# Stacked f32r score products in the first attention, and the value products between the second and third group of turned tiles

## The reference, cut to what matters

```python
h = tok(x)                                   # patches @ W + b + pos_embed
h = concatenate([h, txt], axis=1)            # 1536 tokens x 64
n = layernorm(h)
q, k, v = n @ Wq + bq, n @ Wk + bk, n @ Wv + bv
h = h + softmax(q @ k.T) @ v                 # "attn0": one head of 64
```

## Time and profile before

| what | value |
|---|---|
| median of 3 runs | 5559.78 us (5559.76 to 5568.03) |
| the profiled execution's own time | 5535.23 us |
| its span, first to last instruction | 5533.4 us |
| mean granted TensorE clock | 0.834 of full speed |
| busy: PE, PEld, DVE, ACT, POOL | 78%, 52%, 60%, 34%, 9% of the span |

### The profile page before, as it was taken

The page is one execution under the profiler, slowest core; times in us unless marked ns, Lnnn a source line. Parts: engine busy times, 40 slices in busy tenths (PEclk is TensorE's granted clock), DMA queues, the critical chain, the costliest instruction groups (busy, mean ns, idle before and its releaser), DMA issues.

```text
span 5533.4 us, 72582 instructions
## 1 busy us (share of the span) xinstructions
PE 4295.1 (78%) x26536; PEld 2888.3 (52%) x26536; DVE 3325.1 (60%) x9075; ACT 1894.7 (34%) x3395; POOL 490.8 (9%) x820
## 2 busy tenths in 40 slices
PE   6886855699888855699888855699887855699987
PEld 4554634555646534555646534555646544555646
DVE  4444769555545769555545769555555769655555
ACT  2333522144332522144432522134432532234432
POOL 0110000011100000021100000021100000021100
PEclk9898865699988975699988975689998985699988
DMA  2000000000000000000000000000000000000000
GB/s 81 3 3 16 1 16 1 1 1 1 1 1 4 1 16 1 1 1 1 1 1 4 1 16 1 1 1 1 1 1 4 1 1 1 1 1 1 1 1 4
DMA packets 28333, 26.68 MB, mean 5 GB/s; under 512 B 10550, under 2 KB 26934, under 8 KB 27450
## 3 DMA queue, kind: packets, MB, share of 16 engines
q1 hardware_dynamic: 27962, 21.98, 1.4%
HBM read 20.40 MB, written 1.57 MB: 4 GB/s over the span
## 4 chain that ended last, share of the span: by engine, by line
PE 52%; DVE 30%; POOL 4%; issue 2%; ACT 2%; DVEq 1%; SPq 0%; POOLq 0%; ACTq 0%
PE ps L594 11%; PE ps L630 7%; DVE qup L779 4%; PE ps L657 4%; PE ps L1624 3%; PE ps L1608 3%; DVE x L777 3%; DVE x L781 3%; DVE ctxt L822 3%; DVE ctxt L818 3%; POOL st L395 2%; PE ps L935 2%; PE ps L597 2%; DVE row_max L1067 2%; PE ps L964 2%
## 5 line engine op out<-in xcount | busy, mean ns | idle before, releaser
L630 PE MATMUL ps<-cst,big 128*128 128x128 f32 x4608 | 659.5, 294 | 308.9 <-ACT big L733 251.7
L630 PEld LDWEIGHTS ps<-cst,big 128*128 128x128 f32 x4608 | 567.0, 152 | 366.2 <-ACT big L733 255.7
L713 ACT COPY big<-ps 128x512 f32<-128x512 f32 x816 | 478.5, 586 | 742.4 <-PE ps L630 739.6
L737 ACT ACTIVATE big<-ps,negmax 128x1024 f32<-128x1024 f32 (+1 forms) x672 | 600.1, 899 | 265.7 <-DVE negmax L852 265.7
L852 DVE TENSOR_REDUCE negmax<-ps 128x1 f32<-128x1536 f32 x336 | 590.4, 1758 | 64.6 <-PE ps L601 44.8
L410 PE MATMUL ps<-cst 128*128 128x512 f32 x608 | 334.2, 710 | 127.9 <-DVEq L187 58.2
L594 PE MATMUL ps<-kup,qup 128*128 128x512 f32 (+3 forms) x768 | 355.2, 559 | 41.9 <-POOLq L187 41.1
L395 POOL TENSOR_TENSOR st<-st,cst 128x6 f32<-128x6 f32 x104 | 156.9, 1508 | 2579.5 <-DVE st L383 2575.4
L423 ACT COPY xt<-ps 64x512 f32<-64x512 f32 x144 | 78.4, 580 | 808.6 <-PE ps L415 808.5
L601 PE MATMUL ps<-qlo 128*128 128x512 f32 x576 | 337.9, 725 | 7.5 <-DVEq L187 7.5
L657 PE MATMUL ps<-big,v 128*32 128x128 f32 (+1 forms) x8064 | 321.9, 277 | 8.1 <-DVE ctxt L1091 6.0
(11 more groups left out here) (318 smaller groups left out, 7201.9 us busy)
## 6 DMA issues: line engine op xcount, KB each, us to landing
rw<-in_w_route SPq DMA_DIRECT2D x128, 64.5 KB, 1.9
cst<-in_consts SPq DMA_DIRECT2D x1, 2671.0 KB, 14.9
cst<-in_consts SPq DMA_DIRECT2D x1, 2670.5 KB, 8.9
big<-in_consts SPq DMA_DIRECT2D x1, 1872.5 KB, 22.1
out_dram<-res SPq DMA_DIRECT2D x4, 384.0 KB, 2.8
experts_in<-in_consts SPq DMA_DIRECT2D x1, 1360.0 KB, 17.6
qup<-in_patches SPq DMA_DIRECT2D x4, 260.0 KB
klo<-in_pe_low SPq DMA_DIRECT2D x2, 384.0 KB, 23.6
```

Of the source, the lines that this page charges most:

```text
L630: ins = nc.tensor.transpose(turned_bank(kind, u, g)[:, i * P:(i + 1) * P], prob[:, slot_of(kind, u), (4 * g + i) * P:(4 * g + i + 1) * P], ...
L713: copy(pt[:, slot_of(kind, u), g, 0:n], turned_bank(kind, u, g)[:, 0:n]).then_inc(*ph.mark(copier(kind, g)))
L737: nc.scalar.activation(prob[:, slot_of(kind, u), cols], src[:, cols], ACT.Exp, bias=bias, accum_out=part_sum[:, u, k:k + 1]).then_inc(*ph. ...
```

## The change

In embed, `clear_upper` goes. DVE writes each of the two weight matrices twice side by side into `twice` (two copies of 128 x 128), so a product gives q (or k) twice, on partitions 0 to 63 and 64 to 127. ACT writes the result rounded to f32r (the high part) to all 128 partitions; DVE writes the remainder (the low part): for q on the upper 64 partitions, for k on all 128 into a second slot of `k_stack`. In attn0 a score block is then two f32r products, (q high + q low) with k high and (q high + q low) with k low, accumulated in one bank, in place of one float32 product.

In `attn_pe`, for all attention phases but attn2 and attn4, `context(u - 1)` moves from behind the third `turn` to between the second and the third.

```diff
-        def qkv_pe(ph, pe, wq, wk, wv):
+        def qkv_pe(ph, pe):
             keep_clock(1, 9)
             pe.wait_ge(*ph.after("normed", 1))
             transpose_pe(ph, x, [0, 1, 2])
-            for j in range(NB):
+            pe.wait_ge(*ph.after("weights_spread", 2))
+            for i, (w, j) in enumerate(qkv_blocks()):
                 pe.wait_ge(*ph.after("xt_copied", j + 1))
-                nc.tensor.matmul(ps[0:D, 3 + j, :], W(wq), xt[:, 512 * j:512 * (j + 1)], start=True, stop=True)\
-                    .then_inc(*ph.mark("q_psum"))
-            for j in range(NB):
-                nc.tensor.matmul(ps[0:D, (6 + j) % 8, :], W(wk), xt[:, 512 * j:512 * (j + 1)], start=True, stop=True)\
-                    .then_inc(*ph.mark("k_psum"))
-            rows_pe(ph, W(wv), xt, [1, 2], "v_psum")
+                nc.tensor.matmul(ps[:, (3 + i) % 8, :], twice[:, w, :, :].rearrange("p r d -> p (r d)"), xt[:, 512 * j:512 * (j + 1)], start=True, stop=True)\
+                    .then_inc(*ph.mark("stack_psum"))
+            rows_pe(ph, W("v0"), xt, [1, 2], "v_psum")
...
-            for j in range(NB):
-                act.wait_ge(*ph.after("k_psum", j + 1))
-                nc.scalar.copy(kt[0:D, 512 * j:512 * (j + 1)], ps[0:D, (6 + j) % 8, :])
...
+            for i, (w, j) in enumerate(qkv_blocks()):
+                act.wait_ge(*ph.after("stack_psum", i + 1))
+                nc.scalar.activation((q_stack, k_stack)[w][:, 0, 512 * j:512 * (j + 1)].bitcast(F32R), ps[:, (3 + i) % 8, :],
+                                     ACT.Identity).then_inc(*ph.mark("high_ready"))
+
+        def qkv_vec(ph, dve):
+            for i, (w, j) in enumerate(qkv_blocks()):
+                cols = slice(512 * j, 512 * (j + 1))
+                dve.wait_ge(*ph.after("high_ready", i + 1))
+                if w == 0:
+                    ins = nc.vector.scalar_tensor_tensor(q_stack[D:P, 0, cols].bitcast(F32R), ps[D:P, (3 + i) % 8, :], 1.0,
+                                                         q_stack[D:P, 0, cols], ALU.mult, ALU.subtract)
+                else:
+                    ins = nc.vector.scalar_tensor_tensor(k_stack[:, 1, cols].bitcast(F32R), ps[:, (3 + i) % 8, :], 1.0,
+                                                         k_stack[:, 0, cols], ALU.mult, ALU.subtract)
+                ins.then_inc(*ph.mark("low_ready"))
...
+                elif kind == "attn0":
+                    for part in range(2):
+                        ins = nc.tensor.matmul(bank, q_stack[:, 0, qs].bitcast(F32R), k_stack[:, part, lo * P:hi * P].bitcast(F32R),
+                                               start=(part == 0), stop=(part == 1))
...
-                for g in range(NB):
-                    turn(u, g)
+                turn(u, 0)
+                turn(u, 1)
                 if u > 0:
                     context(u - 1)
+                turn(u, 2)
...
-                clear_upper(ph, pool)
                 norm_pool(ph, pool, 1)
...
+                for w, name in enumerate(("q0", "k0")):
+                    nc.vector.tensor_copy(twice[:, w, :, :], W(name).unsqueeze(1).to_broadcast([P, 2, D]))\
+                        .then_inc(*ph.mark("weights_spread"))
```

More of the change, by code:

```diff
@@ L51 @@
 SIGNALS = {
-    "embed": {"pool_step": 1, "rstd_ready": 2, "xt_copied": 3, "emb_psum": 1, "xt_psum": 3, "q_psum": 3, "k_psum": 3,
+    "embed": {"weights_spread": 2, "rstd_ready": 2, "xt_copied": 3, "emb_psum": 1, "xt_psum": 3, "stack_psum": 6, "high_ready": 6, "low_ready": 6,
         "v_psum": 2, "vec_step": 13, "var_ready": 2, "normed": 1},
@@ L278, in build @@
         work = qup[:, 0, :]
+        twice = big[:, 0:2 * P].rearrange("p (w r d) -> p w r d", w=2, r=2)
         spread = big[:, 0:4 * P].rearrange("p (w h r d) -> p w h r d", w=2, h=2, r=4)
@@ L434, in rows_bank, with qkv_blocks @@
             return ps[:, banks[i], 0:6 * n].rearrange("p (t d) -> p t d", d=n)
-        def qkv_pe(ph, pe, wq, wk, wv):
+        def qkv_blocks():
+            return [(w, j) for j in range(NB) for w in range(2)]
+        def qkv_pe(ph, pe):
             keep_clock(1, 9)
@@ L1394, in _ @@
                 ins.then_inc(*ph.mark("emb_psum"))
-                qkv_pe(ph, pe, "q0", "k0", "v0")
+                qkv_pe(ph, pe)
                 ph.leave(pe)
@@ L1676, in _ @@
                 ready_vec(ph, dve)
-                qkv_vec(ph, dve, 1.0)
+                qkv_vec(ph, dve)
                 ph.leave(dve)
```

## The result

The changed kernel takes 5643.92 us (median of four runs, 5613.52 to 5654.91) beside 5559.77 us of the kernel before: 1.0142 times as long, 95% interval 1.0096 to 1.0189. The forecast was +36 us, 5596, with a range of 5560 to 5630; measured are +84 us, above the range. Each stage figure comes from the one profiled execution of its kernel, so it carries no interval.

What follows compares the result with a forecast made beforehand. No engine bounds the whole span: PE bounds attn0, ACT's near-slackless loop attn1, DVE's loop attn3. Terms +73.6 - 36.0 - 1.5 + 0.4 = +36 us gave 5559.8 + 36 = 5596 us, range 5560 to 5630.

Steps and rivals of the forecast that it cites:

- The bound of each phase: Per unit: PE in attn0 (5.77 us), ACT's loop of 3.32 against 3.39 in attn1, DVE's loop in attn3a (5.84).
- Moved block in attn1, +73.6: attn1: value products enter ACT's loop, 3.32 to 4.25 us per unit; net +18.4 us per sample, +73.6 over four.
- The gap of 0.93: attn1: length taken for the value-product block with its waits, 612.80 - 610.55 - 1.32 = 0.93 us.
- attn0, -36.0: attn0: f32r scores cut PE's work to 4.72 us, the moved order sets 4.87; -9.0 us per sample, -36.0 over four.
- The f32r pair at 0.26: attn0: each of two f32r products accumulated in one bank costs 0.26 us; at 0.45 attn0 would gain nothing.
- rival 3: attn0: the f32r pair is slow, the unit stays at 5.77, only attn1's loss shows: 5636 us; chance 0.05.
- embed, +0.4: embed: two weight copies on DVE, in the open in sample 0 only, cost 0.4 us; the other changes nothing.
- attn3, "-1.5 us", hidden behind the DVE loop: attn3a and attn3b: the block is hidden with 1.6 us to spare, period stays 5.84; eight phases together -1.5 us.
- +0.25, and -0.44 for the tail: attn3, end of each phase: last step follows the later exp, +0.25 us; last context starts four transposes sooner, -0.44.
- Clock 1.00 in all: Sign expected in the profile: granted clock 1.00 in attn0, attn1 and attn3.
- rival 4: attn1: granted clock falls as PE idles some 0.8 us of every 4.25; about +190 us, half the time 5690; chance 0.07.

Runs made afterwards that it cites:

- e1: Changed kernel with the value products back behind the third turn everywhere, f32r scores of attn0 kept: 5502.4 us, 0.9905 of the kernel before.
- e2: Kernel before with only the moved order put in, attn0 keeping its float32 scores: 5656.23 us, 1.0186 of the kernel before.
- e6: e1 with the moved order in attn3 alone: 5520.31 us, 0.9941 of the kernel before.
- e10: Whole change, but the last two of 24 units of each attn3 phase keep the old order: 5602.86 us, 1.0085 of the kernel before.
- e9: e1 with the last unit's turn in each attn3 phase waiting for both halves of the exponentials: 5526.15 us, 0.9958 of the kernel before.
- e5: Whole change plus dummy PE products in waits at the ends of attn3 and ahead of its rotary stage: 5591.17 us, 1.0061 of the kernel before.
- e7: e1 plus dummy PE products at the ends of attn3 and ahead of its rotary stage: 5500.86 us, 0.9914 of the kernel before.
- e4: Changed kernel with the moved order in attn1 alone, f32r scores kept: 5589.82 us, 1.0070 of the kernel before.
- e3: Changed kernel with the moved order in attn0 and attn3 but not attn1, f32r scores kept: 5536.36 us, 0.9969 of the kernel before.
- e8: e1 with attn1's twelve value products cut in two, six before and six behind the third turn: 5561.21 us, 1.0016 of the kernel before.

## Why the prediction was wrong, step by step

- **The bound of each phase.** Right. PE in attn0, ACT's loop with next to no slack in attn1, DVE's loop in attn3, whose steady unit stayed at 5.84.
- **Moved block in attn1, +73.6.** Right: +75.1. Period 4.25 of a forecast 4.25. The gap of 0.93 that I took as the block's length is split otherwise (0.79 for the block, and group 2 alone reaches ACT 0.14 later than as the end of twelve: 1.02 + 0.69 against the 1.57 of the earlier trace rows); from T to the copy it is 2.50 us, 1.57 + 0.93.
- **attn0, -36.0.** Right: -36.0, and to that point by luck, since the terms in it are off and offset each other. Over the four samples the stretch from the first to the last row sum (POOL's addition behind each unit's exps) fell by 25.4 us and not by the 30.0 of the steps forecast, with a period of 4.92 and not 4.87 and a first step of sample 0 at the lower clock; the stretch ahead of the first row sum fell by 8.1 and not by 4.2, the tail by 2.5 and not by 1.8. PE's own work, which does not enter this sum, is 4.59 and not 4.72: a unit's float32 scores are 5.42 / 2 = 2.7 by the earlier trace rows where 2.6 was taken. That makes the split alone worth 51 us (e1).
- **The f32r pair at 0.26.** Right (e1), rival 3 falls.
- **embed, +0.4.** The two weight copies take 0.36 us of DVE; too small to find in a run.
- **attn3, "-1.5 us", hidden behind the DVE loop.** This is the step that failed: +36.4. It split the phase into 22 steps of a hidden loop and a last step that "follows the exp: +0.25, and -0.44 for the tail". The +0.25 was right as a delay, 4.20 from the last unit but one to the last against 3.98 before, and where the clock does not fall it costs no more (e2, 154.0 against 153.8). The prediction priced it at its own length and took the clock as given. In fact it is a further stand-still of PE behind one of more than a microsecond, and behind it, in most ends, the granted clock is the lower one for the turn and the value products, and once more for the first projections of the next phase. Of the 36.4 us, 29.3 lie behind the last row sum of the eight phases (137.9 us in sum, 108.6 before). e6 shows that the order in attn3 alone costs it, e10 that the last two units alone do, e9 that a stand-still of the same place without the order does, e5 that filling it gives it back.
- **"Clock 1.00 in all".** Wrong, and rival 4 looked in the wrong phase. It feared attn1, where PE now idles 0.60 us in every unit; there the clock stayed at 1.00. I had the row that should have warned me, the clock at 0.50 behind a stretch of attn4 in which PE was busy 2.69 of 4 us, and asked only of the loops, not of the ends of phases. The Trainium skill (TensorE: Matmul & The Clock Gate, Part 4: PE-mode transpose) holds that transposes do not count as busy in the way products do. The trace does not bear out the fall that the prediction drew from it: attn1, with 12 transposes in a unit and PE idle besides, kept 1.00 from its second unit to its last join in all four samples.
- **What stays open.** rel3a rose by 11.1 us and attn2's stretch by 6.4. In rel3a it is clock again: behind a wait of 4.16 us and 12 transposes, 24 products take 5.38 us (sample 0), where they took 2.89 before; e5, with seven more dummies in that wait, brings the stage from 95.5 to 80.0, though e7 with the same dummies is slow there in one sample of four. But the kernel before has the same wait at nearly the same length (3.91) and is slow there in one sample, and e1 in three of four; attn3, too, is 6 us longer in e1 and e4 than before, with no edit in it; half of that lies ahead of the first row sum, where in sample 0 the first 7 us of attn3a have a mean clock of 0.55 in e1 and of 0.76 before. So some 6 of the 36.4 us come without the moved order. Why the same wait or the same end costs the clock in one sample and not in another no run here tells: in the four executions with the moved ends unfilled (after, e2, e3, e6) the last turn or its value products ran at the lower clock at 25 of 32 ends. Nor was attn2's share tried. These stages differ by some 10 us between kernels that are alike in them, and that may be part of why the runs of the changed kernel spread over 41 us; that it is was not shown.

In sum: with the ends of attn3 put back, the rest of the change measures 1.0085 (1.0064 to 1.0107), +36 to +59 us, and the forecast of +36 is at its lower edge; the clock at the ends of attn3 makes up most of the difference to +84, 29 us by the stage (1284.7 - 1255.8), and rel3a part of the rest.

The best version measured is e1, the split without the moved order: 0.9905 of the kernel before; by the ratios the change takes 1.0142 / 0.9905 = 1.024 times as long.

## What to carry to other kernels

Before you put work between a producer and the consumer that closes a loop, add up the loop; if its slack is under the length of the work, the period grows by the difference however idle the engine looks. A delay at the end of a phase is priced by what PE does next: look up where PE stands still longest, read the granted clock behind it in every sample and not in one, and treat a few tenths more there as a possible doubling of the work that follows. When two edits come together, measure each alone: here the one gave 50 us and the other took over 100.

## What the runs showed of the hardware that was not expected

- A stand-still of 1.27 us, a join and immediate work kept the clock at 1.00 through the last turn and its value products at all 40 ends of before, e1, e4, e8 and e10. With 1.12 us, the join and 0.26 us more it fell to 0.50 there at 25 of 32 ends (after, e2, e3, e6), with 1.27 us, the join and 0.72 us more at 7 of 8 (e9), and with dummies in the wait at none of 16 (e5, e7). Averaged over all eight phases that costs 24.6 / 8 = 3.1 us in e9 against e1, and 27.0 / 8 = 3.4 in e6, several times the delay that sets it off.
- Dummy products made the whole change faster by 0.8% of its time, and did nothing where the clock was not lost (e7).
- PE waiting 0.60 us in each 4.25 us, with 12 transposes in the rest, kept 1.00 from attn1's second unit to its last join.
- Six value products between transposes took 0.57 us, twelve 0.79.
